# Two heads to a 32-row quarter of the weighing's output, and the weighing ranked behind the passes

## The reference, cut to what matters

```python
q = rope(x @ W_Q.T); k = rope(x @ W_K.T); v = x @ W_V.T       # 16 heads of 8 features each
scores = einsum('bhqd,bhkd->bhqk', q, k) / sqrt(8)
scores = where(causal, scores, -inf)
attn = softmax(scores, axis=-1)
out = einsum('bhqk,bhkd->bhqd', attn, v)                       # the "weighing"
x = x + out.reshape(16, 256, 128) @ W_O.T
```

## Time and profile before

| | |
|---|---|
| median of 3 runs | 667.73 us (667.33 to 671.45) |
| the profiled execution | 668.1 us, span 666.3 us |
| PE busy | 631.2 us, 95% of the span |
| DVE busy | 495.0 us, 74% |
| ACT busy | 495.1 us, 74% |
| POOL busy | 298.8 us, 45% |
| mean granted clock of TensorE | 0.996 of full speed |

### The profile page before, as it was taken

How to read it: one execution, slowest core, us unless ns; L and a number is a source line. 1 busy time by engine, 2 the same in 40 slices (tenths; PEclk the granted TensorE clock), 3 DMA queues, 4 the chain that set the end, 5 groups by cost and what they waited for, 6 DMA issues and landing times.

```text
span 666.3 us, 14363 instructions
## 1 busy us (share of the span) xinstructions
PE 631.2 (95%) x5343; PEld 475.8 (71%) x5343; DVE 495.0 (74%) x1300; ACT 495.1 (74%) x846; POOL 298.8 (45%) x461
## 2 busy tenths in 40 slices
PE   4899999999999999999999999989999999999995
PEld 3587878888887878887778887655555666666664
DVE  6767566585586686686798667999898898888655
ACT  5799688788888788787788677337777777777870
POOL 1402111330331535231574563767878745655661
PEclk9999999999999999999999999989999999999999
DMA  9200000000000002000011144442434322221001
GB/s 301 89 0 1 1 0 1 1 0 1 1 0 1 0 18 79 1 1 1 0 49 48 49 139 177 143 144 78 144 123 137 95 93 94 74 72 40 20 9 41
DMA packets 41886, 37.80 MB, mean 57 GB/s; under 512 B 2940, under 2 KB 37020, under 8 KB 41816
## 3 DMA queue, kind: packets, MB, share of 16 engines
q1 hardware_dynamic: 41816, 36.87, 17.6%
HBM read 21.92 MB, written 14.68 MB: 55 GB/s over the span
## 4 chain that ended last, share of the span: by engine, by line
PE 66%; DVE 17%; ACT 9%; issue 5%; POOL 1%; DMA 0%; DVEq 0%; ACTq 0%; POOLq 0%
PE PSA L940 19%; PE PSA L944 19%; PE PSA L1142 6%; DVE MX L1334 5%; PE PSA L959 3%; DVE G L1206 3%; PE PSA L1095 2%; PE PSA L1129 2%; PE PSA L1079 2%; ACT PSA L1380 2%; PE PSA L1072 2%; PE PSA L1151 1%; ACT G L1376 1%; DVE RA L1327 1%; PE PSA L1102 1%
## 5 line engine op out<-in xcount | busy, mean ns | idle before, releaser
L940 PE MATMUL PSA<-ah,WH 128*128 128x512 f32 x320 | 130.0, 406 | 1.5 <-DVE al L1211 0.9
L1334 DVE TENSOR_REDUCE MX<-PSA 128x6 f32<-128x768 f32 x128 | 118.3, 949 | 15.7 <-PE PSA L1102 15.1
L1380 ACT ACTIVATE PSA<-PSA,SC 128x512 f32<-128x512 f32 x128 | 84.7, 662 | 55.0 <-PE PSA L944 54.3
L944 PE MATMUL PSA<-al,WH 128*128 128x512 f32 x320 | 125.2, 391 | 0.0
L1469 ACT ACTIVATE PB<-PSA 128x768 f32<-128x768 f32 x128 | 99.0, 813 | 17.9 <-PE PSA L1129 16.8
L940 PE MATMUL PSA<-bh,WH 128*128 128x512 f32 x256 | 104.8, 409 | 2.7 <-DVE G L1206 2.3
L1552 POOL TENSOR_SCALAR_AFFINE_SELECT PB<-PB 128x512 f32<-128x512 f32 x128 | 79.5, 635 | 51.7 <-ACT PB L1469 50.3
L944 PE MATMUL PSA<-bl,WH 128*128 128x512 f32 x256 | 100.3, 392 | 0.0
L1498 POOL TENSOR_SCALAR VE<-MV 128x4 f32<-128x4 f32 x46 | 10.9, 236 | 194.7 <-DVE MV L1181 194.7
L1211 DVE TENSOR_TENSOR al<-PSA,ah 128x512 fp32r<-128x512 f32 x64 | 44.0, 687 | 52.6 <-ACT ah L1387 52.2
L940 PEld LDWEIGHTS PSA<-ah,WH 128*128 128x128 f32 x320 | 60.2, 188 | 14.8 <-DVE al L1211 2.2
(11 more groups left out here) (148 smaller groups left out, 1321.0 us busy)
## 6 DMA issues: line engine op xcount, KB each, us to landing
KS<-dk SPq DMA_DIRECT2D x32, 192.0 KB
QS<-dq SPq DMA_DIRECT2D x32, 192.0 KB
...
```

The source lines that it names most:

```text
L940: e.matmul(o, WH[:, col:col + 128], hi, start=first, stop=False)
L944: return e.matmul(o, WH[:, col:col + 128], low, start=False, stop=last)
L1334: e.tensor_reduce(MX[:, u % 2, 1:4, :].rearrange("p t (l g) -> p l t g", l=2)[:, :, :, g], PSA[:, b:b + 2, 0:384].rearrange("p l (t k) -> ...
L1380: e.activation(bank(b), bank(b), ACT.Gelu, scale=SC[:, k:k + 1]).then_inc(a_gelu, 1)
```

## The change

Heads 2v and 2v+1 of a group of eight go to the same 32-row quarter v. `VA` of the first has its features in columns 0 to 7 and ones in 8 to 15, and zeros in the other 16 columns; the second has zeros first, features in 16 to 23 and ones in 24 to 31. The multiplications of "weigh" (even g) and "weighed" (odd g) are accumulated into the same bank, so a quarter ends up with both heads, and only after "weighed" ACT copies the bank. `OT` has two parts in place of four, one "upright" step of 4 transposes takes both halves of the tokens, DVE's reciprocal takes 32 values and its product 256 columns. The order of the heads in W_Q, W_K and in the cosines is permuted to match, on the host. `WEIGH` is 6.5 in place of 5.9, "max_out" counts as a quarter step for the planner, and "peak" of a sequence isn't planned before the "max_out" of the one ahead of it.

```diff
--- before.py
+++ after.py
@@ -78,7 +78,8 @@
     "pass1": [("P", 0.29, 0.46), ("V", 0.868, 0.95)], "peak": [("V", 0.14, 0.22), ("A", 0.13, 0.24), ("G", 0.2, 0.26)],
     "max_out": [("P", 0.22, 0.29), ("V", 0.2, 0.27), ("S", 1.18, 1.18), ("D", 3.8)],
     "pass2": [("P", 0.17, 0.34), ("A", 0.69, 0.81), ("G", 0.59, 0.63)],
-    "weigh": [("P", 0.69, 0.78), ("A", 0.27, 0.38)], "upright": [("P", 0.45, 0.6), ("V", 0.5, 0.58)],
+    "weigh": [("P", 0.69, 0.78)], "weighed": [("P", 0.69, 0.78), ("A", 0.27, 0.38)],
+    "upright": [("P", 0.45, 0.6), ("V", 0.65, 0.73)],
     "flat": [("P", 0.27, 0.44), ("A", 0.27, 0.38)], "proj": [("P", 0.64, 0.71), ("V", 0.33, 0.41)], "store": [("S", 0.9, 0.9)],
     "half_stat": [("V", 0.7, 0.8)], "half_power": [("G", 1.1, 1.1)], "half_norm": [("V", 0.45, 0.5)], "half_xt": [("P", 0.2, 0.6), ("A", 0.27, 0.38)],
     "half_logit": [("P", 0.2, 0.4), ("V", 0.5, 0.6)], "half_tanh": [("A", 0.09, 0.2)], "half_pick": [("V", 1.3, 1.4)],
@@ -89,11 +90,11 @@
 COMES = {"stat": [3.5], "cast_v": [5.6, 12.6], "cast_a": [7.1, 8.5, 10.6]}
 
 BESIDE = ("norm",)
-TILES = {"pass1": "h", "pass2": "h", "weigh": "q"}
+TILES = {"pass1": "h", "pass2": "h", "weigh": "q", "weighed": "q", "max_out": "q"}
 TABLES = {"silu": "silu", "gelu": "gelu", "pass2": "exp"}
 AHEAD = 0.0
 STAY = 0.0
-WEIGH = 5.9
+WEIGH = 6.5
 KEPT = 5
 SLOTS = 8
 QUEUED = 1.0
@@ -573,7 +574,10 @@
 
     def maxima(self, u, p1):
         yield from self.until(p1.done - 0.3)
+        while self.hmfree is None:
+            yield
         pk = self.put("peak", u=u, src=p1, emptied=self.hmfree)
+        self.hmfree = None
         yield from self.until(pk.done)
         b, free = yield from self.sr.get(self)
         mx = self.put("max_out", u=u, b=b, emptied=free, src=pk)
@@ -610,13 +614,18 @@
             while len(ps) < 2 * g + 2:
                 yield
             yield from self.until(ps[2 * g + 1].done)
-            while self.otfree[u % 2] is None:
+            if g % 2 == 0:
+                while self.otfree[u % 2] is None:
+                    yield
+                b, free = yield from self.sr.get(self)
+                w = self.put("weigh", u=u, g=g, b=b, emptied=free)
+            else:
+                w = self.put("weighed", u=u, g=g, b=b, emptied2=self.otfree[u % 2], src=w)
+                self.otfree[u % 2] = [] if g < 3 else None
+                self.sr.free[b] = [w]
+            self.pbfree[2 * g % SLOTS] = self.pbfree[(2 * g + 1) % SLOTS] = [w]
+            if g < 3:
                 yield
-            b, free = yield from self.sr.get(self)
-            w = self.put("weigh", u=u, g=g, b=b, emptied=free, emptied2=self.otfree[u % 2])
-            self.otfree[u % 2] = [] if g < 3 else None
-            self.sr.free[b] = [w]
-            self.pbfree[2 * g % SLOTS] = self.pbfree[(2 * g + 1) % SLOTS] = [w]
         self.turn["weigh"] += 1
         self.vfree[u % KEPT] = [w]
         self.add(6.6, self.fin(u, w))
@@ -625,12 +634,10 @@
         yield from self.until(w.done)
         while self.vqfree[u % 2] is None:
             yield
-        out, vqfree, self.vqfree[u % 2] = [], self.vqfree[u % 2], None
-        for h in range(2):
-            b, free = yield from self.sr.get(self)
-            o = self.put("upright", u=u, h=h, b=b, emptied=free, emptied2=vqfree, src=w)
-            self.sr.free[b] = [o]
-            out.append(o)
+        vqfree, self.vqfree[u % 2] = self.vqfree[u % 2], None
+        b, free = yield from self.sr.get(self)
+        o = self.put("upright", u=u, b=b, emptied=free, emptied2=vqfree, src=w)
+        self.sr.free[b] = [o]
         self.otfree[u % 2] = [o]
         while self.vcfree[u % 2] is None:
             yield
@@ -791,10 +798,10 @@
             KS[n] = sb(f"KS{n}", [128, 8, S], BF16)
             VA[n] = sb(f"VA{n}", [128, 2, NH, 32])
         PB = sb("PB", [128, SLOTS, 3, 2, 128])
-        OT = [sb(f"OT{n}", [128, 4, S]) for n in range(2)]
+        OT = [sb(f"OT{n}", [128, 2, S]) for n in range(2)]
         VC = sb("VC", [128, 2, S])
         VQ = sb("VQ", [128, 2, 2, 128])
-        RC = sb("RC", [128, 2, NH])
+        RC = sb("RC", [128, 2, 2 * NH])
         PSA = ctx.enter_context(nc.psum_tensor("PSA", [128, 8, 512], F32))
         DQ = nc.dram_tensor("dq", [NB, 6, 2, 8, 8, S], BF16)
         DKK = nc.dram_tensor("dk", [NB, 6, 2, 8, 8, S], BF16)
@@ -916,7 +923,7 @@
                     w.wait_ge(v_mx, m)
                 elif st.name == "pass2":
                     w.wait_ge(a_prob, m)
-                elif st.name == "weigh":
+                elif st.name == "weighed":
                     w.wait_ge(a_ot, m)
                 elif st.name == "upright":
                     w.wait_ge(v_vq, m)
@@ -1131,25 +1138,27 @@
                                          Q[64 * h:64 * h + 52, g, 128 * k:256], start=(k == 0), stop=True,
                                          skip_group_check=True)
                     t.then_inc(p_pass2, 1)
-                elif st.name == "weigh":
-                    V = VA[u % KEPT]
+                elif st.name in ("weigh", "weighed"):
+
+                    V, a = VA[u % KEPT], g % 2
                     w.wait_ge(g_sel, 8 * u + 2 * g + 2)
                     w.wait_ge(a_vexp, u + 1)
                     emptied(w, st.emptied)
                     for k in range(2):
                         for v in range(4):
                             P = PB[:, (2 * g + v // 2) % SLOTS, :, v % 2, :]
-                            t = e.matmul(PSA[32 * v:32 * v + 32, b, 128 * k:256], V[:, k, 4 * g + v, :],
-                                         P[:, 1, :] if k else P[:, 0::2, :], start=(k == 0), stop=(k == 1))
+                            t = e.matmul(PSA[32 * v:32 * v + 32, b, 128 * k:256], V[:, k, 8 * (g // 2) + 2 * v + a, :],
+                                         P[:, 1, :] if k else P[:, 0::2, :], start=(k == 0 and a == 0),
+                                         stop=(k == 1 and a == 1), skip_group_check=True)
                     t.then_inc(p_weigh, 1)
                 elif st.name == "upright":
 
-                    w.wait_ge(a_ot, st.src.n + 1)
+                    w.wait_ge(a_ot, 2 * u + 2)
                     w.wait_ge(s_id, 16)
                     emptied(w, st.emptied)
                     for q in range(4):
-                        t = e.transpose(PSA[:, b, 128 * q:128 * q + 128], OT[u % 2][:, q, 128 * st.h:128 * st.h + 128],
-                                        IDN[:, :])
+                        t = e.transpose(PSA[:, b, 128 * q:128 * q + 128],
+                                        OT[u % 2][:, q % 2, 128 * (q // 2):128 * (q // 2) + 128], IDN[:, :])
                     t.then_inc(p_up_right, 1)
                 elif st.name == "flat":
                     w.wait_ge(v_vq, st.src.n + 1)
@@ -1346,14 +1355,15 @@
                         w.wait_ge(s_m[(u - 2) % KEPT], 32 * ((u - 2) // KEPT + 1))
                     e.tensor_copy(MT[:, u % 2, :], PSA[0:32, b, 0:128].bitcast(BF16)).then_inc(v_mt, 1)
                 elif st.name == "upright":
-                    O = bank(b).rearrange("p (m r) -> p m r", r=32)
+                    O = bank(b).rearrange("p (m r) -> p m r", r=16)
                     w.wait_ge(p_up_right, n + 1)
-                    e.reciprocal(RC[:, st.h, :], O[:, :, 8]).then_inc(v_rc, 1)
+                    w.wait_ge(v_vq, n - 1)
+                    e.reciprocal(RC[:, u % 2, :], O[:, :, 8]).then_inc(v_rc, 1)
                     w.wait_ge(v_rc, n + 1)
                     for s in st.emptied2:
                         w.wait_ge(p_flat, s.n + 1)
-                    e.tensor_tensor(VQ[:, u % 2, st.h, :].rearrange("p (m r) -> p m r", r=8), O[:, :, 0:8],
-                                    RC[:, st.h, :].rearrange("p (m o) -> p m o", o=1).to_broadcast([128, NH, 8]),
+                    e.tensor_tensor(VQ[:, u % 2, :, :].rearrange("p t (m r) -> p (t m) r", r=8), O[:, :, 0:8],
+                                    RC[:, u % 2, :].rearrange("p (m o) -> p m o", o=1).to_broadcast([128, 2 * NH, 8]),
                                     ALU.mult).then_inc(v_vq, 1)
 
         def scalar(e, w):
@@ -1456,16 +1466,16 @@
                     w.wait_ge(a_value, st.src.n + 1)
                     w.wait_ge(s_one[u % KEPT], 16)
                     for s in st.emptied:
-                        if s.name == "weigh":
-                            w.wait_ge(p_weigh, s.n + 1)
-                    e.activation(VA[u % KEPT][:, :, :, 0:8],
-                                 VS[:, 2 * u:2 * u + 2, :].rearrange("p k (h d) -> p k h d", h=NH),
+                        if s.name == "weighed":
+                            w.wait_ge(p_weigh, 4 * s.u + s.g + 1)
+                    e.activation(VA[u % KEPT][:, :, :, :].rearrange("p k (m a) (b r) -> p (k m) (a b) r", a=2, b=2)[
+                        :, :, 0::3, 0:8], VS[:, 2 * u:2 * u + 2, :].rearrange("p k (m a d) -> p (k m) a d", a=2, d=8),
                                  ACT.Copy).then_inc(a_vexp, 1)
```

(15 more changed lines are left out.)

## The result

| | before | changed |
|---|---|---|
| median of 6 runs each, same chips | 669.77 us (667.33 to 671.45) | 661.39 us (660.98 to 662.75) |
| ratio, 95% interval | | 0.9884 (0.9859 to 0.9910) |
| profiled execution, its span | 668.1, 666.3 us | 661.4, 659.7 us |

Whether it reaches the 1% that the prediction took as its bound is not settled: the ratio 0.9884 does and the upper end 0.9910 does not, and the median, 661.39, lies just over the 661.1 that it had named. The forecast was 659.2, from a kernel before at 667.7, so a gain of 8.5 us. Its median here is 669.77, so the medians alone (8.4 us) would flatter the forecast; the ratio times 668 us gives a gain of 7.7 us, the two profiled spans 6.6.

The account below looks back on a forecast made before the run. TensorE, 95% busy, was taken as the bound; transposes -7.0, tile shapes -1.3, gaps -2.6 and tail +2.4 sum to -8.5 us, from 667.7 to 659.2 us. The range was 655.5 to 663.6 us.

Parts of the forecast that it names:

- the 1% that the prediction took as its bound: Whole kernel: a measurement tells about 1%, 6.7 us, from no change; faster means under 661.1 us, slower over 674.4.
- The bound: From 456 to 648 us: TensorE bounds the kernel, so time taken from its work comes off the span nearly whole.
- DVE "counted at nothing": DVE's finish, beside the path: fewer reciprocals and products relieve DVE of 6.4 us, counted as no gain.
- The rival in which DVE is the bound up to 600 us: Up to 600 us DVE takes over as bound: gain only 4.2, 663.5 us; DVE's share stays 88% or rises; chance 0.10.
- ACT "counted at nothing": ACT's copies after the weighing, beside the path: 32 of 64 go, 12.3 us, hidden by TensorE's work, no gain.
- The sum up to the last weighing: First to last weighing: transposes -7.0, tile shapes -1.3 and gaps -2.6 bring the last weighing about 11 us earlier.
- Gaps: TensorE between first and last weighing: 32 fewer filling multiplications at 0.08 us each, -2.6 us, ends 1.8 and 6.1.
- more than the forecast: Rival at the weighing's weight loads: half of the 7.4 us waits for POOL's triangle go too, 655.5 us; chance 0.08.
- its own test: TensorE, 450 to 640 us: the prediction is wrong on the whole if unfilled idle time grows beyond 7.9 us.
- Transposes and tile shapes as busy time: TensorE, on the path: 64 of 128 transposes go, -7.0 us; fewer changes of tile shape, -1.3 us.
- The tail: After the last upright: four picks on DVE instead of three, a loss of 2.4 us, ends 0 and 3.1.
- Late weighings holding the slots: Rival: later weighings hold PB's slots, delaying the next exponential and TensorE, 0.27 us each, +8.8, 676.5 us; chance 0.04.

Follow-up runs that it names:

- the version that goes further: Changed kernel with planner DVE costs raised, WEIGH 6.7, LEAD 18, last two sequences' finish ranked 4: 660.05 us, ratio 0.9857.
- putting all three back: Changed kernel with transposes, ACT's copies and DVE's reciprocals and products all done twice: 683.33 us, ratio 1.0237.
- the packing alone: Changed kernel with WEIGH back at 5.9, so weighings are ranked ahead of pass2 as before: 662.84 us, ratio 0.9904.
- the rank alone: Kernel before with WEIGH 6.5, still one head to a quarter, 128 transposes and 64 copies: 668.69 us, ratio 0.9994.
- The pick fewer: Changed kernel with the last three sequences' finish ranked 4, so three picks follow the last upright instead of four: 660.60 us, ratio 0.9883.

## Why the prediction came near, and where it was wrong

The forecast of 659.2 us, a gain of 8.5, came near the measured 6.7 to 7.7 us partly by luck: TensorE's microseconds were priced too high, and the gains on DVE and ACT, counted at nothing, made up for it.

- **The bound: wrong, and this is the step that failed.** "A microsecond taken from TensorE's work between 456 and 648 us should therefore come off the span nearly whole." The kernel before without 64 transposes gained 2.1 us, where the sum gives 7.0. The same number put back into the changed kernel cost 4.2. The sentence rests on the earlier trace rows, where the weight loads wait only for POOL, 7.4 us; their waits for DVE's maxima, 2.6 and 4.2 us, were left out.
- **DVE "counted at nothing": wrong.** A microsecond is worth most there. At 0.7 to 1.0 us for each, the relief of 4.8 us is worth an estimated 3.6 to 4.6, if work taken off counts like work put on. The rival in which DVE is the bound up to 600 us had its mark in the profile after, as the prediction had written it down: DVE's share there stayed at 88% (132.5 of 150). But the mark tells little. The share lies between 130.8 and 133.1 of 150 in every kernel here but the version that goes further (134.7), and so also with ACT's copies twice (130.9), where DVE has nothing more to do and the kernel is 8.2 us longer. Nor does the rival's sum hold with the sizes as measured: 0.30 us of relief for ten sequences, 2.6 for TensorE behind 600 and 3.9 lost in the tail leave 1.7 us of gain.
- **ACT "counted at nothing": wrong.** ACT waits for TensorE before the copies, so the copies looked covered. But ACT's queue is in a fixed order too: by the order, the exponentials behind a copy are late by it, and pass2 and POOL behind them. At 0.3 us a microsecond, the 12.0 us fewer copies are worth an estimated 3.6.
- **The sum up to the last weighing: right, from wrong terms.** Forecast -10.9, measured -10.5. By the experiments, estimated, 4.6 for DVE, 3.6 for ACT and 2.1 for the transposes make 10.3. That these shares simply add up was not shown, and putting all three back cost less than the single costs together. The close fit is partly chance: the packing alone gained 6.4 us in the whole with 1.2 us lost in the tail (19.7 for 18.5), so about 7.6 in the middle, and the rank alone brought the last weighing 2.9 us forward, which leaves no room for 10.3 from the packing.
- **Gaps: wrong.** -2.6 was taken, -0.3 came. POOL's triangle does hold TensorE for 3.4 us less, which is what the case "more than the forecast" had hoped for, but the waits on the maxima grew by 3.8. The prediction had named its own test: wrong on the whole if the unfilled idle time of TensorE from 450 to 640 us grows beyond its present 7.9 us. (7.9 is the figure of 450 to 650 us; up to 640 it was 190 less 182.5 = 7.5.) It grew, to 190 less 178.5 = 11.5 us, and between the first and the last weighing from 7.4 to 10.8; the row of the changed kernel is this:

```profile
450.00:640.00 190.00, 178.54 (x2797) 111.73 (x2796) 159.42 (x374) 141.95 (x257) 132.79 (x219) 1.00 0.28 85
```

- **Transposes and tile shapes as busy time: nearly right.** The upright group fell from 17.8 to 10.1 us, by 7.7. As the transposes' own time the term of 7.0 is borne out: without 64 of them the group of the kernel before is 11.0 us, 6.8 less, and twice over that of the changed kernel is 17.1, 7.0 more. But TensorE's whole work moved by only 5.1 and 5.0 us with them. So of the 10.1 us of work that left the stretch, 5.1 to 7.7 are transposes, and 2.4 to 5.0 what is left for tile shapes and all else, where 1.3 had been worked out. The price of 0.11 to 0.14 us a change was not tried alone.
- **The tail: right in kind, too small.** 2.4 forecast, 3.9 measured, over the upper end of 3.1. The pick fewer gives 1.7 back. Another 1.0 is in DVE's idle time ahead of a pick, rows in order of time behind the last upright of the changed kernel:

```profile
641.04 0.15 DVE L1314 TENSOR_SCALAR GS<-TT 128x1 f32<-128x1 f32 x1 [1.05 <-issue]
...
648.21 0.15 DVE L1314 TENSOR_SCALAR GS<-TT 128x1 f32<-128x1 f32 x1 [1.01 <-ACT TT L1424]
...
651.69 0.15 DVE L1314 TENSOR_SCALAR GS<-TT 128x1 f32<-128x1 f32 x1 [1.09 <-issue]
...
654.80 0.15 DVE L1314 TENSOR_SCALAR GS<-TT 128x1 f32<-128x1 f32 x1 [0.73 <-issue]
```

  Three of four idle for 1.0 to 1.1 us and not for the 0.68 and 0.73 of the earlier trace rows, 1.0 us in all; one of the three ends with a wait for ACT. It is not the whole cause: the packing alone has three picks behind its last upright, idles for only 0.67 to 0.73 us ahead of each, and still takes 18.2 us from its last reciprocal to the end, for 16.5 before. What makes up the rest is open.
- **Late weighings holding the slots: rightly set aside.** All of the exponentials' waits, 24.0 us, are for pass2 on TensorE. That they grew from 10.4 was not foreseen. It comes with the packing: the packing alone has 27.3 us of these waits, the rank alone 10.7. It isn't that ACT, with fewer copies to do, stands earlier before the next exponential, since with each copy done twice the waits are still 22.8. The cause is open.
